# A decoder's attention kernel on one core: where the row-maxima blocks stand between TensorE's other blocks, and over how many PSUM banks they go

## The chip, the core and the metric

The kernel runs on one core of a Trainium2 chip. The metric is the device time in microseconds (us), the median of three runs. One further execution was taken by the hardware profiler; its trace is what the rows below show. TensorE is called PE (PEld is its weight load), VectorE DVE, ScalarE ACT, GpSimd POOL, and SyncE SP.

## What is computed

Two decoder layers with a layer norm ahead of each part, on x of 4 x 512 x 256:

```
x = x + self_attention0(norm(x))      # 16 heads of 16, all 512 keys, bias min(slope*(q-k), 8)
x = x + cross_attention0(norm(x), ctx, mask)   # 8 heads of 64, 1601 keys, keys masked
x = x + mixture0(norm(x))
x = x + attention1(norm(x))           # over the 4 batch entries, causal
x = x + cross_attention1(norm(x), ctx)         # 16 heads of 64, 1601 keys, no mask
x = x + mixture1(norm(x))

sim = q @ k.T * scale ;  attn = softmax(sim, -1) ;  out = (attn @ v) @ Wo + bo
```

All is float32; the softmax needs the maximum over the keys for each query row.

## The kernel before, in words

Each stage is a block in which every engine runs its own hand-written instruction list, and the engines meet at semaphores. An engine takes its list strictly in order, so an instruction that waits holds up all that stands behind it.

In both attention kinds the scores are computed twice. First, with the queries on the partitions, only for the row maximum: PE writes scores into a bank MB, DVE reduces the bank to one number per query. These are the **maxima**. Later, with the keys on the partitions and minus the maximum folded into the product as one more row, for the softmax: PE writes **scores** into one of three banks SB, ACT takes the exponential into a ring PR, PE multiplies PR with the values into OB (the **values**). The maxima of a group run while the scores of the group before it are worked on.

**Self attention** (`self_attention`): 256 score tiles n of 128 x 512, 16 of them are a group (4 heads, 4 query tiles). The loop over n has on PE: scores n (L617), the jobs of `at(n)`, the maxima of tile n + 22 (L581) and, at each fourth n, the values (four products side by side, L593). At n % 16 == 6 PE turns the finished output of the group before (L601) in its own bank OB. DVE's loop has a band subtraction on part of the scores (L751), the jobs, the maxima (L720 with a bias strip, L723 without) and, at n % 16 == 8, the division. Jobs are the projections "p" and "v", the row job that turns the maxima, and "a" and "o" for the output; they share the one bank JB, and each waits until the one before has been read. Banks: three SB, two MB, two OB, one JB.

**Cross attention** (`cross`, layer 0 masked with 4 pairs of heads, layer 1 without mask and 8 pairs): a group g is one pair of heads of one batch entry, 16 groups in layer 0 and 32 in layer 1. A group has 14 steps t over its 13 key tiles. On PE a step is: scores of head 0 and head 1 (L1077 and L1078 each), the jobs of `at(g, t)`, one **couple** of maxima, the values of the step before (L1093), and another couple. A couple is the maxima matmul (L1050) of head 0 into MB[0] and that of head 1 into MB[1], 400 keys wide, for one query tile. A group needs 16 couples, two in each step t = 3 to 10, for the group after. On DVE a step is the jobs, the four reductions (L1217 masked, L1220 not), then at t = 3 to 6 one quarter of the reciprocal of the sums (L1227), with the product (L1231) behind the last. Jobs: "k" (L1009, ACT copies the high half, DVE subtracts for the low half, L1191) at t = 0 to 3, "q" at 0, "sum" at 2, "v" (L1021, ten matmuls) from 4 on in most groups, "out" (L1036) at 8 and 9, "row" (L1025) at 11. Not every step has a "v" job: in layer 1 an even group has it at t = 4 to 7, an odd one at 4 to 6; for the last two pairs of a batch entry (an even and an odd group) all seven lie in the odd one. The groups 6, 14, 22 and 30 of layer 1 and 2, 6, 10 and 14 of layer 0 thus have no job at t = 4 to 7. Layer 0 also prepares the next batch entry's mask on DVE in three groups. PE may write a maxima bank once DVE has reduced what was in it: maxima m waits for reduction m - 2.

## Times and profile before

| | us |
|---|---|
| median of 3 runs | 3410.16 |
| lowest, highest | 3408.29, 3428.79 |
| the profiled execution | 3417.53 |
| its span in the trace | 3415.8 |
| mean granted TensorE clock, share of full | 0.926 |

| engine | busy us | share of the span |
|---|---|---|
| PE | 2995.6 | 88% |
| PEld | 1748.6 | 51% |
| DVE | 1934.0 | 57% |
| POOL | 1675.4 | 49% |
| ACT | 1274.2 | 37% |

A busy PE is one with a matmul in its pipeline; the ends are modelled, so the start of a matmul against the start of the next says more than its duration. Self attention lies at about 160 to 560 us of the span, the masked cross attention at 600 to 1500, the other one at 1700 to 3275.

### The profile page before, as it was taken

The page shows a single profiled execution, that of the slowest core. Times are in us where ns is not written, and L with a number is a line of the kernel's source. Part 1 is how long each engine was busy: PE and PEld are TensorE (multiplying, and loading weights), DVE is VectorE, ACT ScalarE, POOL GpSimd, SP SyncE. Part 2 cuts the span into 40 slices and gives each one's busy share as a digit, 9 for nine tenths or more (in the row PEclk, how much of TensorE's full clock was granted, in tenths as well). Part 3 has the DMA queues.
Part 4 walks back from the last instruction along what each step waited for, and adds up shares of the span by engine and source line. Part 5 has one row for each costly group of instructions (what it writes and reads, how often), then busy time and mean ns, then how long its engine had stood idle before and what let it go on. Part 6 is the DMA issues. An engine that isn't in the chain of part 4 may idle for free. (4 is left out here: it accounts for less than half of the span.)

```text
span 3415.8 us, 38759 instructions
## 1 busy us (share of the span) xinstructions
PE 2995.6 (88%) x12634; PEld 1748.6 (51%) x12634; DVE 1934.0 (57%) x4250; ACT 1274.2 (37%) x2299; POOL 1675.4 (49%) x1408
## 2 busy tenths in 40 slices
PE   6578886889999899768589999999999999999979
PEld 5223333555555455354355555555555555555557
DVE  2455664565665665443555665565556555655546
ACT  1144443434344344311144444444444444444420
POOL 0344202355555656530246665666656666666620
PEclk8778886999999999888599999999999999999979
DMA  8756501233132222100222232222312223222110
GB/s 270 149 158 152 114 1 61 66 93 71 40 94 65 74 69 51 37 0 0 65 64 57 70 94 57 56 70 62 91 48 70 68 55 84 70 62 54 40 50 25
DMA packets 113536, 245.84 MB, mean 72 GB/s; under 512 B 15366, under 2 KB 61703, under 8 KB 112184
## 3 DMA queue, kind: packets, MB, share of 16 engines
q1 hardware_dynamic: 107128, 219.82, 25.6%
q0 software_dynamic: 5696, 23.42, 2.5%
q8 instruction: 102, 1.67, 0.2%
q14 instruction: 98, 0.80, 0.1%
q10 hardware_dynamic: 512, 0.13, 0.0%
HBM read 107.31 MB, written 31.76 MB: 41 GB/s over the span
## 5 line engine op out<-in xcount | busy, mean ns | idle before, releaser
L991 POOL TENSOR_TENSOR ACC<-ACC,PR 128x512 f32<-128x512 f32 (+1 forms) x1056 | 1346.1, 1296 | 636.6 <-ACT PR L1162 636.4
L1162 ACT ACTIVATE PR<-bank 128x512 f32<-128x512 f32 (+1 forms) x832 | 452.1, 595 | 783.5 <-PE bank L1078 780.1
L1093 PE MATMUL bank<-PR,V 128*64 128x512 f32 (+1 forms) x2496 | 665.5, 616 | 0.9 <-ACT OT L1148 0.7
L1050 PE MATMUL bank<-KH,QZ 128*128 128x400 f32 (+1 forms) x1536 | 529.3, 404 | 113.8 <-DVE mx L1220 57.4
L1220 DVE TENSOR_REDUCE mx<-bank 128x1 f32<-128x400 f32 (+1 forms) x1024 | 538.8, 567 | 145.5 <-PE bank L1050 134.2
L1077 PE MATMUL bank<-QA,KA 128*128 128x512 f32 (+1 forms) x1248 | 534.5, 428 | 4.6 <-DMA QB<-ROW 4.6
L1050 PEld LDWEIGHTS bank<-KH,QZ 128*128 128x128 f32 x1536 | 269.7, 190 | 503.9 <-DVE mx L1220 306.1
L1191 DVE TENSOR_TENSOR KB<-bank,KH 64x400 fp32r<-64x400 f32 (+1 forms) x384 | 219.6, 572 | 531.0 <-ACT KH L1121 527.3
L1078 PE MATMUL bank<-QB,KB 65*128 65x512 f32 (+1 forms) x1248 | 498.2, 399 | 0.0
L1162 ACT ACTIVATE PR<-bank,keybias 128x512 f32<-128x512 f32 (+1 forms) x416 | 264.3, 683 | 406.7 <-PE bank L1078 395.7
L1077 PEld LDWEIGHTS bank<-QA,KA 128*128 128x128 f32 (+1 forms) x1248 | 232.9, 187 | 213.5 <-issue 94.7
L1217 DVE CUSTOM_DVE_ANT_0 bank<-bank,maskadd 128x400 f32<-128x400 f32 (+1 forms) x512 | 284.8, 593 | 66.6 <-PE bank L1050 63.9
L991 POOL TENSOR_TENSOR ACC<-PR 128x512 f32<-128x512 f32 x96 | 121.4, 1284 | 289.8 <-ACT PR L1162 289.8
L1078 PEld LDWEIGHTS bank<-QB,KB 65*128 65x128 f32 (+1 forms) x1248 | 233.7, 187 | 41.8 <-issue 11.0
L1093 PEld LDWEIGHTS bank<-PR,V 128*64 128x64 f32 (+1 forms) x2496 | 128.3, 135 | 203.1 <-issue 131.0
L1021 PEld LDWEIGHTS bank<-WV,CX 128*128 128x128 f32 (+1 forms) x1560 | 209.2, 188 | 15.1 <-issue 0.4
L1009 PE MATMUL bank<-CX,WK 128*128 128x400 f32 (+1 forms) x960 | 209.6, 349 | 8.4 <-DVE KB L1191 5.4
L1021 PE MATMUL bank<-WV,CX 128*128 128x256 f32 (+1 forms) x1560 | 214.9, 283 | 0.0
L679 ACT ACTIVATE PR<-bank 128x512 f32<-128x512 f32 x256 | 146.3, 598 | 183.2 <-DVE bank L751 130.1
L1227 DVE RECIPROCAL RD<-RD 128x128 f32<-128x128 f32 x192 | 180.0, 942 | 47.6 <-ACT RD L1113 46.7
L1009 PEld LDWEIGHTS bank<-CX,WK 128*128 128x128 f32 x960 | 180.5, 191 | 26.6 <-DVE KB L1191 6.7
L1205 DVE TENSOR_TENSOR X<-bank,X 128x512 f32<-128x512 f32 x96 | 66.4, 691 | 152.3 <-PE bank L1036 152.3
(228 smaller groups left out, 3110.0 us busy)
## 6 DMA issues: line engine op xcount, KB each, us to landing
KA<-KH SPq DMA_DIRECT2D x192, 400.5 KB, 6.3
CX<-ctx_split SPq DMA_DIRECT2D x8, 2403.0 KB, 10.6
WK<-wk_split SPq DMA_DIRECT2D x48, 256.0 KB, 5.7
WV<-wv_split SPq DMA_DIRECT2D x24, 512.0 KB, 3.6
QA<-QZ SPq DMA_DIRECT2D x96, 128.0 KB, 2.3
QB<-QZ SPq DMA_DIRECT2D x96, 128.0 KB, 2.4
first<-in_w_in SPq DMA_DIRECT2D x8, 1024.0 KB, 6.3
second<-in_w_out1T SPq DMA_DIRECT2D x8, 1024.0 KB, 8.8
```

The source lines that it names most:

```text
L991: pool.tensor_tensor(acc, other, PR[0:r, n % RING, :], ALU.add).then_inc(summed, 1)
L1009: last = pe.matmul(J[:, 0:w], W[:, u, :], CX[:, v, o:o + w], start=(n == 0), stop=(n == 4))
L1021: last = pe.matmul(J[0:r, o:o + 2 * P], CX[:, v, t * P:t * P + r], WV[:, u, :], start=(n == 0), stop=(n == 4))
L1050: pe.matmul(MB[h][:, 0:w], QZ[:, h, t * P:(t + 1) * P], KH[:, o:o + w], start=True, stop=True).then_inc(mx_ready, 1)
L1077: pe.matmul(SB[n % 3][0:r, :], KA[:, par, h, t * P:t * P + r], QA[:, par, h, :], start=True, stop=False)
L1078: pe.matmul(SB[n % 3][0:r, :], KB[:, par, h, t * P:t * P + r], QB[:, par, h, :], start=False, stop=True).then_inc(sc_ready, 1)
L1093: last = pe.matmul(OB[h * DH:(h + 1) * DH, :], V[0:r, g % 4, s, h * DH:(h + 1) * DH], PR[0:r, (n + h) % RING, :], start=(s == 0), stop=(s ...
L1162: act.activation(PR[0:r, n % RING, :], SB[n % 3][0:r, :], ACT.Exp, bias=keybias[0:r, g // pairs, t:t + 1] if masked else 0.0).then_inc(pro ...
L1191: last = dve.tensor_tensor(KB[0:DH, par, h, o:o + w], J[hd, 0:w], KH[hd, o:o + w], ALU.subtract)
L1217: dve.tensor_tensor_reduce(MB[h][:, 0:w], MB[h][:, 0:w], maskadd[:, g // pairs % 2, o:o + w], 1.0, -BIG, ALU.add, ALU.max, out).then_inc(m ...
L1220: dve.tensor_reduce(out, MB[h][:, 0:w], AX.X, ALU.max).then_inc(mx_done, 1)
L1227: dve.reciprocal(part, part).then_inc(inverted, 1)
```

## The change

One PSUM tensor `banks` of eight banks takes the place of eight tensors; `bank[i]` is a slice of it. Then:

- Self attention: three banks for the maxima (maxima m waits for reduction m - 3) and one OB in place of two. The turning of a finished output becomes a job "turn" in the bank JB, at n % 16 == 6, ahead of that step's maxima in place of behind them; the division reads JB and stands one step earlier on DVE. The values of a group wait until ACT has copied the output of the group before. The "p" jobs stand at 1, 3, 17, 19 of a batch entry's 64 steps (2, 5, 18, 21 before), the second "o" pair at 25 and 29 (24 and 26).
- Cross attention: the 32 maxima of a group stand in steps 2 to 9 (3 to 10 before), four in a step. Masked: one behind the scores of head 0, one behind those of head 1, one behind the jobs, one behind the values. Not masked: a pair between the scores of the two heads and a pair behind the jobs, none behind the values; DVE takes both heads by one reduction over the two banks (128 x 2 x 400), and PE waits for the reduction of the pair before. DVE has two of its reductions (masked) or one (not masked) ahead of the jobs of the step, the rest behind.

```
-        self.bank = [ctx.enter_context(nc.psum_tensor(f"bank{i}", [P, 512], F32)) for i in range(8)]
+        self.banks = ctx.enter_context(nc.psum_tensor("banks", [P, 8, 512], F32))
+        self.bank = [self.banks[:, i, :] for i in range(8)]
...
-        SB, MB, OB, JB = bank[0:3], bank[3:5], bank[5:7], bank[7]
+        SB, MB, OB, JB = bank[0:3], bank[3:6], bank[6], bank[7]
...
+            if n % GN == 6 and n >= GN:
+                jobs.append(("turn", n // GN - 1, 0))
...
-                        if m >= 2:
-                            pe.wait_ge(mx_done, m - 1)
+                        if m >= 3:
+                            pe.wait_ge(mx_done, m - 2)
...
-                        if t == 0 and g >= 2:
-                            pe.wait_ge(o_done, g - 1)
+                        if t == 0 and g >= 1:
+                            pe.wait_ge(o_raised, g)
...
-        def couples(g, t):
+        def singles(g, t):
 
-            return [(g + 1, i) for i in range(2 * (t - 3), 2 * (t - 2))] if g + 1 < G and 3 <= t <= 10 else []
+            return [(g + 1, i, h) for i in range(2 * (t - 2), 2 * (t - 1)) for h in range(2)] if g + 1 < G and 2 <= t <= 9 else []
...
+                        m = 2 * (NT * NC * g + i) + h
+                        turn = m // 2 if h == 0 and not masked else m - 1
...
+                        if m >= 2 and (masked or h == 0):
+                            pe.wait_ge(mx_done, turn)
+                        pe.matmul(MB[h][:, 0:w], QZ[:, h, t * P:(t + 1) * P], KH[:, o:o + w],
+                                  start=True, stop=True).then_inc(mx_ready, 1)
...
+                                for x in singles(g, t)[h:h + 1] if masked else singles(g, t)[0:2 - 2 * h]:
+                                    maximum(*x)
                             for x in at(g, t):
                                 job(x)
-                            for x in couples(g, t)[0:1]:
-                                maxima(*x)
+                            for x in singles(g, t)[2:3] if masked else singles(g, t)[2:4]:
+                                maximum(*x)
...
-                                dve.tensor_reduce(out, MB[h][:, 0:w], AX.X, ALU.max).then_inc(mx_done, 1)
+                            dve.tensor_reduce(mx[:, :, t, c], both[:, :, 0:w], AX.X, ALU.max).then_inc(mx_done, 1)
```

PE in the second cross attention, an odd group, steps 7 and 8 (no "v" job in step 7), before. KH, QZ are the maxima; QA, KA and QB, KB the scores; PR, V the values; WO, OT the "out" job:

```order
L1077 MATMUL bank<-QA,KA 128x512
L1078 MATMUL bank<-QB,KB 128x512
L1077 MATMUL bank<-QA,KA 128x512
L1078 MATMUL bank<-QB,KB 128x512
L1050 MATMUL bank<-KH,QZ 128x400 x2
L1093 MATMUL bank<-PR,V 64x512 x2
L1050 MATMUL bank<-KH,QZ 128x400 x2
L1077 MATMUL bank<-QA,KA 128x512
L1078 MATMUL bank<-QB,KB 128x512
L1077 MATMUL bank<-QA,KA 128x512
L1078 MATMUL bank<-QB,KB 128x512
L1036 MATMUL bank<-WO,OT 128x256 x2
```

The same step 7 and the start of step 8 in the change:

```order
L1074 MATMUL banks<-QA,KA 128x512
L1075 MATMUL banks<-QB,KB 128x512
L1046 MATMUL banks<-KH,QZ 128x400 x2
L1074 MATMUL banks<-QA,KA 128x512
L1075 MATMUL banks<-QB,KB 128x512
L1046 MATMUL banks<-KH,QZ 128x400 x2
L1092 MATMUL banks<-PR,V 64x512 x2
L1074 MATMUL banks<-QA,KA 128x512
L1075 MATMUL banks<-QB,KB 128x512
L1046 MATMUL banks<-KH,QZ 128x402 x2
```

Between the two pairs of a step there were the values; now there is one head's scores and the job, if there is one, and the values lie between the second pair and the next step.

DVE in the second cross attention, from the "k" job of step 3 to the end of step 7, before. KB is the subtraction of the "k" job, mx the reductions, RD and OT the reciprocal and the product:

```order
L1191 TENSOR_TENSOR KB<-bank,KH 64x402 x2
L1220 TENSOR_REDUCE mx<-bank 128x1 x4
L1227 RECIPROCAL RD<-RD 128x128
L1220 TENSOR_REDUCE mx<-bank 128x1 x4
L1227 RECIPROCAL RD<-RD 128x128
L1220 TENSOR_REDUCE mx<-bank 128x1 x4
L1227 RECIPROCAL RD<-RD 128x128
L1220 TENSOR_REDUCE mx<-bank 128x1 x4
L1227 RECIPROCAL RD<-RD 128x128
L1231 TENSOR_TENSOR OT<-OT,RD 128x512
L1220 TENSOR_REDUCE mx<-bank 128x1 x4
L1205 TENSOR_TENSOR X<-bank,X 128x512
```

In the change:

```order
L1190 TENSOR_TENSOR KB<-banks,KH 64x402 x2
L1220 TENSOR_REDUCE mx<-banks 128x2
L1227 RECIPROCAL RD<-RD 128x128
L1220 TENSOR_REDUCE mx<-banks 128x2 x2
L1227 RECIPROCAL RD<-RD 128x128
L1220 TENSOR_REDUCE mx<-banks 128x2 x2
L1227 RECIPROCAL RD<-RD 128x128
L1220 TENSOR_REDUCE mx<-banks 128x2 x2
L1227 RECIPROCAL RD<-RD 128x128
L1231 TENSOR_TENSOR OT<-OT,RD 128x512
L1220 TENSOR_REDUCE mx<-banks 128x2 x3
```

Four reductions of one bank became two of two banks; the first of step 3 now stands ahead of the "k" job, and the first "out" addition behind the first pair of step 8.

PE in self attention around the turning of an output, before (QS, KS with L617 scores, KS, QS with L581 maxima):

```order
L617 MATMUL bank<-QS,KS 128x512
L581 MATMUL bank<-KS,QS 128x512
L601 MATMUL bank<-ident,RAISED 128x128 x4
L617 MATMUL bank<-QS,KS 128x512
L581 MATMUL bank<-KS,QS 128x512
L593 MATMUL bank<-PR,SV 32x512 x4
```

In the change:

```order
L617 MATMUL banks<-QS,KS 128x512
L570 MATMUL banks<-ident,RAISED 128x128 x4
L587 MATMUL banks<-KS,QS 128x512
L617 MATMUL banks<-QS,KS 128x512
L587 MATMUL banks<-KS,QS 128x512
L599 MATMUL banks<-PR,SV 32x512 x4
```

The turning moved from behind the maxima to ahead of them.

## Rows read from the trace of the kernel before

**Rows 1.** Stages in the windows view: length, engines' busy us (instructions), TensorE clock, DMA

```profile
160.00:560.00 400.00, 329.00 (x1305) 132.81 (x1305) 226.81 (x629) 176.33 (x321) 103.44 (x124) 0.78 0.41 96
600.00:1500.00 900.00, 807.74 (x3421) 477.68 (x3421) 530.31 (x1396) 371.37 (x623) 516.35 (x411) 0.95 0.25 62
1700.00:3275.00 1575.00, 1493.77 (x6544) 874.58 (x6544) 921.66 (x1590) 655.00 (x1227) 985.08 (x781) 1.00 0.27 65
```

**Rows 2.** Timeline, second cross attention, one ordinary step: start us, duration, instruction

```profile
2624.42 0.64 PE L1050 MATMUL bank<-KH,QZ 128*128 128x400 f32 x2
2624.89 0.39 PE L1077 MATMUL bank<-QA,KA 128*128 128x512 f32 x1
...
2625.83 1.34 PE L1021 MATMUL bank<-WV,CX 128*128 128x256 f32 x10
2625.88 0.94 DVE L1227 RECIPROCAL RD<-RD 128x128 f32<-128x128 f32 x1
...
2627.00 0.53 PE L1050 MATMUL bank<-KH,QZ 128*128 128x400 f32 x2
2627.39 1.05 DVE L1220 TENSOR_REDUCE mx<-bank 128x1 f32<-128x400 f32 x2 [0.56 <-PE bank L1050]
2627.46 1.08 PE L1093 MATMUL bank<-PR,V 128*64 128x512 f32 x4
2628.47 0.45 PE L1050 MATMUL bank<-KH,QZ 128*128 128x400 f32 x1
```

**Rows 3.** Timeline, step 3 of a group: the reductions behind the "k" job

```profile
2619.45 2.18 DVE L1220 TENSOR_REDUCE mx<-bank 128x1 f32<-128x400 f32 x4
...
2620.09 0.93 PE L1050 MATMUL bank<-KH,QZ 128*128 128x400 f32 x2 [1.02 <-DVE mx L1220]
2620.86 0.39 PE L1077 MATMUL bank<-QA,KA 128*128 128x512 f32 x1
```

**Rows 4.** Timeline, step 7 of an odd group, behind reciprocal and product

```profile
2585.47 1.08 PE L1093 MATMUL bank<-PR,V 128*64 128x512 f32 x4
2585.94 1.26 DVE L1231 TENSOR_TENSOR OT<-OT,RD 128x512 f32<-128x512 f32 x1
2587.12 2.16 DVE L1220 TENSOR_REDUCE mx<-bank 128x1 f32<-128x400 f32 x4
2587.74 0.93 PE L1050 MATMUL bank<-KH,QZ 128*128 128x400 f32 x2 [1.19 <-DVE mx L1220]
```

**Rows 5.** Timeline, the second couple of step 9 and the "row" job of step 11

```profile
2644.81 0.89 PE L1050 MATMUL bank<-KH,QZ 128*128 128x402 f32 x2
...
2600.81 0.30 PE L1025 MATMUL bank<-ident,MT 128*128 128x128 f32 x1 [0.36 <-DVE MT L1237]
```

**Rows 6.** Groups by form: busy us, mean ns of one, idle before

```profile
L1220 DVE TENSOR_REDUCE mx<-bank 128x1 f32<-128x400 f32 x768 | 403.7, 567 | 107.3 <-PE bank L1050 99.1
L723 DVE TENSOR_REDUCE MT<-bank 128x1 f32<-128x512 f32 x80 | 54.0, 684 | 3.7 <-PE bank L581 2.9
```

**Rows 7.** Windows around step 7 of two masked groups without "v" jobs; columns as in Rows 1

```profile
755.00:759.00 4.00, 2.47 (x10) 0.96 (x10) 3.95 (x9) 1.26 (x2) 3.24 (x3) 1.00 0.90 341
759.00:763.00 4.00, 4.00 (x13) 2.97 (x13) 1.31 (x5) 1.37 (x2) 2.06 (x2) 0.57 0.12 50
1173.00:1177.00 4.00, 2.44 (x10) 0.99 (x10) 3.95 (x9) 1.15 (x2) 2.99 (x3) 1.00 0.86 351
1177.00:1181.00 4.00, 3.92 (x17) 2.27 (x16) 2.84 (x10) 1.27 (x2) 2.51 (x2) 1.00 0.04 14
```

**Rows 8.** Timeline, self attention, one block of four scores

```profile
348.55 0.50 PE L617 MATMUL bank<-QS,KS 63*128 63x512 f32 x2
349.32 0.70 DVE L720 CUSTOM_DVE_ANT_0 bank<-bank,strip 128x512 f32<-128x512 f32 x1 [0.89 <-PE bank L581]
...
352.20 0.50 PE L617 MATMUL bank<-QS,KS 63*128 63x512 f32 x2
```

**Rows 9.** Waits within 160 to 560 us: total us, times, longest

```profile
DVE bank L720 <- PE bank L581: 31.1, 38, 2.3
PE bank L581 <- DVE MT L720: 27.4, 43, 1.9
```

94 lines of the change are left out of this document (43 added, 51 removed).

## The prediction

> **What bounds the kernel now.** I read the windows view by stage first. In the second cross attention PE is busy 1494 of 1575 us at a clock of 1.00, in the masked one 808 of 900 at 0.95, in self attention 329 of 400 at 0.78 [rows 1]; DVE stands at 53 to 59% in all three. So PE's list, in its order, sets the length, and DVE matters only where PE waits for it. The next view is the timeline of one ordinary step of the second cross attention. By starts, it is: the second couple of the step before 0.47 us, two heads' scores 0.94, the "v" job 1.17, the first couple 0.46, the values 1.01; 4.05 in all [rows 2]. Four reductions and a reciprocal, 1.05 + 1.05 + 0.94, are done meanwhile, so there is no wait. The waits sit in a few steps of each group:
>
> - Step 3: DVE first does the subtraction of the "k" job. The second couple waits 1.02 us, to which 0.07 belongs that the modelled end of the values covers (they last 1.08 but free PE after 1.01), and its two matmuls take 0.77 in place of 0.47: 1.4 us lost [rows 2, 3].
> - Step 7 of an odd group, which has no "v" job: behind the fourth reciprocal and the product of 1.26 the values' start and the couple's lie 2.27 apart instead of 1.01. With the slower couple that is 1.6 us [rows 4]. With a "v" job of 1.17 in that step 0.4 is left.
> - Steps 8 and 9: the couple lasts 0.89 in place of 0.64, 0.25 us each; step 11: the row job idles 0.36 for the last maxima [rows 2, 5].
>
> **One reduction over two banks.** The trace has none, but a reduction of 400 takes 567 ns and one of 512 takes 684 [rows 6], 1.04 ns an element, so 800 should take 567 + 417 = 984 ns. The bounds are 833 (elements at that rate alone) and 1134 (two of today's); I take 0.98. Its successor starts 0.08 earlier than its end, as behind the product [rows 4].
>
> The Trainium skill ("VectorE: DVE Perf Modes", the section on the TRN2 errata) says that each instruction pays a fixed cost and gives 120 cycles plus one an element at 0.96 GHz for a PSUM source, so one reduction in place of two would save 0.125 us a pair. The row of 567 ns is 25 ns above that formula.
>
> What counts for PE is another thing. A matmul starts about 0.06 us after the reduction that frees its bank (2619.45 + 0.57 = 2620.02, the couple at 2620.09) [rows 3], and before, head 0's bank was free after the first 0.57. Now both banks stay closed until the one reduction is done. With the first matmul of a pair at 0, the second at 0.18 (I take half of an undisturbed pair without a change of block kind, 0.36), a reduction starts 0.39 behind its matmul [rows 2], at 0.57, ends at 1.55, and the next pair can start at 1.61. PE reaches the second pair of a step after 0.36 + 0.47 for the pair and one head's scores, plus the job: at 0.83 + job. From the second pair to the first of the next step there are 0.46 + 1.01 + 0.57 (scores behind values pay 0.1 for the change of kind that the couple pays now) = 2.04 us, always enough unless DVE is busy otherwise.
>
> **Second cross attention, step by step.**
> - Steps with a "v" job of 1.17: 2.00 against 1.61, no wait, 4.05 as before.
> - Step 3 to 4: DVE starts the second pair's reduction where it starts the first one's today, at 2619.45 [rows 3]; the first couple stood at 2617.53 (2620.09 less the wait of 1.02, the values' 1.08 and the couple's 0.46), so that is 1.92 after the "k" job. It ends at 2.91, and the next pair is due at 2.04: 0.93 lost plus 0.1 for the spread of the pair. Gain 0.36 a group.
> - Step 7: behind step 6's second pair DVE has 0.57 + 0.90 (reduction), 0.98 (reciprocal, start to start), 1.19 (product, 2585.94 to 2587.12 [rows 4]); the two-bank reduction starts at 3.64 and ends at 4.62, the next pair starts at 4.68. PE is there at 2.04 + 0.83 + job: with a "v" job 0.64 + 0.1 lost against 0.4; without one 1.8 + 0.1, and 0.3 in step 6 with its half job, against 1.6. Loss 0.35 or 0.6 a group.
> - Steps 8 and 9: 0.4 a group gained. Step 11: 0.36 gained, since the maxima end two steps earlier. The maxima that move from step 10 to step 2 stand between blocks of the other kind there and cost 0.35 more in changes of kind.
> - Groups 6, 14, 22, 30 have no "v" job in steps 4 to 7: each of these steps waits 1.61 - 0.83 = 0.8 + 0.1 (step 4 some 0.3 more), where today they lose about 0.15. That is 2.1 us a group in sum with the other terms.
> - The 16 couples of the first group run alone: two of them with a "v" job take 1.61 + 0.36 + 1.17 = 3.14, at least 2 x 1.61 = 3.2; today four reductions and the waits, some 2.95. Loss 2 us.
>
> Sum: 15 groups with a job in step 7 gain 0.4 (6), 12 odd groups gain 0.1 (1), 4 lose 2.1 (8), 2 at the start: 3 us longer.
>
> **The clock.** In step 7 without a job PE will be idle about 1.8 us. In the masked stage two such steps leave PE busy 2.47 and 2.44 us in 4; after one of them the clock falls to 0.57 in the next 4 us, after the other it stays [rows 7]. That stage's mean is 0.95. In the second cross attention it never falls, with waits like that of [rows 4] in it. With 4.68 us between two second pairs of which 2.87 are work, the new step is emptier than both kinds, and it comes 12 + 4 = 16 times. I take 11 falls. One fall costs at most 4 x 0.43 = 1.7 us [rows 7], less where PE waits anyway: 1.5. That is 16 us, bounds 0 and 27.
>
> **Masked cross attention.** Reductions stay single; only the places change. Step 3's 1.4 shrinks to 0.7, steps 8 and 9 and the row job gain about as above; but the third maxima matmul is now due before the values, 1.0 us earlier against DVE, so steps without a job wait for DVE's reciprocal: four groups lose 1.6, eleven gain 0.4 to 1.2. Sum 2 us gained, and two falls of the clock more (3 us): 1 us longer, bounds -6 and +8.
>
> **Self attention.** In a block of four scores, 3.65 us, DVE idles 0.89 because PE, between the values of 1.0 us, can put only two maxima ahead [rows 8]. A third bank lets it put three: 3 x 0.65 us of DVE work against about 1.8 until the next arrives. DVE's waits of this kind sum to 31 us, and PE's waits the other way to 27 [rows 9]. Not all return: in blocks with projections or at half clock PE itself is the slow one. I take 22 us gained, bounds 0 and 50 (64 blocks by 0.8). What it costs: the turning now stands ahead of the maxima and waits for ACT's copy, and it shares JB. If DVE had nothing in store that is up to 0.7 us in 15 groups, 10 us; with the third bank it has something in store. The moves of "p" and "o" exchange places of equal work: nothing, cover being the exponentials of three banks. No DMA is moved or added.
>
> **Sum.** -22 + 3 + 16 + 1 = -2 us against the profiled execution's 3417.5 us, which stands 0.2% above the median of 3410.2. So 3408.
>
> **Rivals.** About 1% (34 us) is what a measurement of this kernel can tell from no change.
> - *No change beyond 1%*, as forecast: chance 0.62, 3376 to 3444, its likely part 3385 to 3430.
> - *Self attention was bound by the two banks all over*: each block gives back 0.7, 45 us, and steadier work lifts its clock of 0.78. For it: 0.89 idle of DVE in 3.65. Against it: that wait occurs 38 times, not 64. Time 3410 - 45 + 20 = 3385, with the clock 3370. Chance 0.16.
> - *The saved fixed cost comes out in the end*: 512 x (2 x 0.567 - 0.984) = 77 us of DVE work, time 3335. Against it: DVE is 59% busy and has no wait in the ordinary step. Chance 0.03. This is what the skill's rule on fixed costs suggests; its own figure would give 512 x 0.125 = 64 us, as an estimate.
> - *Slower: the two-bank reduction makes the clock fall.* If all 16 step-7 waits and the waits of 0.9 us in the four poor groups bring falls, each costing 1.7 and a late restart of DVE's work, some 30 falls make 51 us, time 3410 - 13 + 51 = 3448 with half the gain in self attention. It decides from about 25 falls on. For it: the emptier step. Chance 0.12.
> - *The one output bank and the turn job hold self attention up*, no gain there: 3430 at 10 us of loss and all else as forecast. Chance 0.07, inside 1% for the most part.
>
> Faster 0.2, same 0.66, slower 0.14. The range 3372 to 3440 leaves out the second rival's lower end, the third and the fourth.
>
> **What would show it.** In the changed profile: a two-bank reduction of 980 ns; in step 7 of odd groups a PE wait of 1.8 us behind the scores, not behind the values; clock below 1.00 between 1700 and 3275; ordinary steps of 4.05 us; no DVE idle of 0.9 behind the values in self attention and a stage some 20 us shorter; a row job without a wait. Wrong would be the prediction if the ordinary step changed its length, since it comes some 150 times, or if self attention moved by more than 40 us.

## The result and the profile after

| | before | after |
|---|---|---|
| median, us | 3411.14 | 3354.52 |
| lowest, highest | 3408.29, 3428.79 | 3353.41, 3356.66 |
| span of the profiled execution | 3415.8 | 3351.8 |
| granted TensorE clock | 0.926 | 0.932 |

The ratio is 0.9837, with a 95% interval of 0.9803 to 0.9871: 1.6% faster. The forecast was 3408, with a range down to 3372. The time lies below the range.

The stages can be told apart by starts: self attention from its first exponential to its last, a cross attention from the row job of its first group to that of its last. The profiled executions give:

| us | before | after | change | forecast |
|---|---|---|---|---|
| self attention | 365.2 | 325.1 | -40.1 | -22 |
| masked cross attention | 767.8 | 764.1 | -3.7 | +1 |
| between the cross attentions | 336.3 | 342.6 | +6.3 | +2 |
| second cross attention | 1506.1 | 1483.3 | -22.8 | +17 |
| the rest | 440.4 | 436.7 | -3.7 | 0 |

The stretch between ends with the row job of the second cross attention's first group, so it holds that group's 16 couples, which run alone (the forecast's "2 at the start" stands here). From the first maxima matmul of that group to its row job, in the windows view (columns: window, length, PE, PEld, DVE, ACT and POOL busy, granted clock, DMA share, GB/s), before and after:

```profile
1700.00:1726.10 26.10, 20.27 (x98) 15.09 (x98) 18.58 (x35) 3.96 (x7) 8.54 (x13) 0.87 0.49 117
1651.20:1683.30 32.10, 20.68 (x97) 16.18 (x97) 17.56 (x19) 3.96 (x7) 8.51 (x13) 0.79 0.40 96
```

PE is busy as long as before and the stretch is 6 us longer. It takes 32.1 to 32.2 us in every run below whose second cross attention reduces two banks at once, and 26.0 to 26.2 us in every other one. So the 6.3 us belong to the two-bank reduction; 2 were forecast. The half clock that falls into it, 6.8 us before and 13.6 after, is part of that.

The stage windows, which answer to [rows 1] (same columns):

```profile
160.00:520.00 360.00, 289.06 (x1305) 121.57 (x1304) 227.36 (x642) 174.81 (x322) 103.89 (x124) 0.87 0.45 108
560.00:1460.00 900.00, 796.73 (x3412) 473.65 (x3412) 548.40 (x1412) 380.64 (x622) 517.27 (x411) 0.95 0.24 61
1650.00:3210.00 1560.00, 1483.41 (x6544) 861.65 (x6544) 869.98 (x1078) 680.38 (x1229) 972.67 (x783) 0.99 0.27 65
```

Self attention's clock rose from 0.78 to 0.87; the second cross attention's, where 11 falls were forecast, is 0.99, and this window also takes in 10 us of half clock around the stage's start.

Groups by form, second cross attention (busy us, mean ns of one, idle before), for [rows 6]:

```profile
L1220 DVE TENSOR_REDUCE mx<-banks 128x2 f32<-128x800 f32 x370 | 365.3, 987 | 155.5 <-PE banks L1046 152.6
L1220 DVE TENSOR_REDUCE mx<-banks 128x2 f32<-128x802 f32 x124 | 122.8, 990 | 60.3 <-PE banks L1046 60.3
```

The two-bank reduction takes 0.987 us; 0.984 was worked out. The Trainium skill ("VectorE: DVE Perf Modes", the section on the TRN2 errata) would give (120 + 800) / 0.96 = 958 ns as an estimate, 3% below the row.

Step 7 of an odd group, without a "v" job, for [rows 4] (timeline: start, duration, instruction, idle before and what ended it):

```profile
1858.86 0.94 DVE L1227 RECIPROCAL RD<-RD 128x128 f32<-128x128 f32 x1
...
1859.83 0.69 DVE L1231 TENSOR_TENSOR OT<-OT,RD 128x512 f32<-128x512 f32 x1
...
1860.37 2.50 POOL L987 TENSOR_TENSOR ACC<-ACC,PR 128x512 f32<-128x512 f32 x2 [1.24 <-ACT PR L1161]
1860.44 0.98 DVE L1220 TENSOR_REDUCE mx<-banks 128x2 f32<-128x800 f32 x1
...
1861.48 0.63 PE L1046 MATMUL banks<-KH,QZ 128*128 128x400 f32 x2 [1.07 <-DVE mx L1220]
1862.05 1.08 PE L1092 MATMUL banks<-PR,V 128*64 128x512 f32 x4
```

PE waits behind the scores, as forecast, but 1.07 us and not 1.8, since the product lasts 0.69 us and not 1.26. The wait behind the "k" job, for [rows 3], and the row job, for [rows 5] (same timeline):

```profile
1846.37 0.99 DVE L1220 TENSOR_REDUCE mx<-banks 128x2 f32<-128x800 f32 x1
...
1847.51 0.60 PE L1046 MATMUL banks<-KH,QZ 128*128 128x400 f32 x2 [0.86 <-DVE mx L1220]
...
1873.76 0.27 PE L1021 MATMUL banks<-ident,MT 128*128 128x128 f32 x1
```

By the starts of the exponentials, the steps of a group of the second cross attention last (median over the groups of a kind, us; "poor" are 6, 14 and 22, without "v" jobs; "single" is the kernel of e7_single_reduce, below):

| step | 2 | 3 | 4 | 5 | 6 | 7 | 8 | 9 | 10 | 11 | group |
|---|---|---|---|---|---|---|---|---|---|---|---|
| even, before | 3.93 | 5.18 | 4.04 | 4.05 | 4.04 | 4.57 | 3.99 | 3.99 | 2.88 | 2.73 | 49.07 |
| even, after | 4.97 | 3.81 | 5.14 | 4.05 | 4.05 | 4.20 | 3.76 | 3.76 | 2.14 | 2.20 | 47.72 |
| even, single | 4.97 | 3.79 | 4.97 | 4.05 | 4.05 | 4.05 | 3.74 | 3.74 | 2.14 | 2.20 | 47.34 |
| odd, before | 3.90 | 5.17 | 4.06 | 4.04 | 3.45 | 4.54 | 3.99 | 4.00 | 2.88 | 2.73 | 48.39 |
| odd, after | 4.98 | 3.80 | 5.14 | 4.04 | 3.75 | 4.21 | 3.77 | 3.76 | 2.14 | 2.18 | 47.43 |
| odd, single | 4.98 | 3.79 | 4.97 | 4.05 | 3.45 | 3.97 | 3.74 | 3.72 | 2.14 | 2.18 | 46.63 |
| poor, before | 3.93 | 5.18 | 3.00 | 3.04 | 3.00 | 4.55 | 4.00 | 3.99 | 2.88 | 2.73 | 45.96 |
| poor, after | 4.97 | 3.81 | 4.90 | 3.75 | 3.75 | 4.22 | 3.76 | 3.76 | 2.14 | 2.20 | 46.92 |
| poor, single | 4.97 | 3.79 | 4.86 | 3.46 | 3.45 | 3.66 | 3.75 | 3.74 | 2.14 | 2.20 | 45.67 |

The ordinary step with a job did not change (4.05).

Self attention: one block of the bias-strip kind, from the score that ends the block before it to the one that ends it, for [rows 8] (timeline):

```profile
339.48 0.50 PE L617 MATMUL banks<-QS,KS 63*128 63x512 f32 x2
...
340.25 0.70 DVE L717 CUSTOM_DVE_ANT_0 banks<-banks,strip 128x512 f32<-128x512 f32 x1 [0.29 <-PE banks L587]
...
342.48 0.50 PE L617 MATMUL banks<-QS,KS 63*128 63x512 f32 x2
```

The block takes 3.00 us (3.65 before), with 0.29 of DVE idle where 0.89 was. The waits of the stage (total us, times, longest), for [rows 9]:

```profile
PE banks L570 <- ACT RAISED L662: 25.2, 13, 3.6
DVE banks L717 <- PE banks L587: 21.6, 32, 1.5
...
PEld banks L587 <- DVE MT L717: 9.8, 25, 3.0
...
PE banks L587 <- DVE MT L717: 2.6, 1, 2.6
```

PE's wait for the reductions fell from 27.4 us to 2.6, and that of its weight loads, which overlaps with it, from the 55.8 of this row of before to 9.8:

```profile
PEld bank L581 <- DVE MT L720: 55.8, 65, 2.6
```

In their place stands the turn job's wait for ACT's copy, 25.2 us. These rows alone don't say from which of the change's parts the 40 us come.

The clock fell once between 1700 and 3160 us, in step 4 of group 22, a poor one (windows, columns as above), for [rows 7]:

```profile
2754.60:2758.60 4.00, 2.47 (x10) 1.26 (x8) 3.44 (x5) 1.19 (x2) 2.08 (x3) 1.00 0.88 178
2758.60:2762.60 4.00, 4.00 (x12) 1.83 (x10) 2.03 (x3) 0.56 (x1) 0.96 (x1) 0.57 1.01 228
```

That group took 48.5 us, the three like it 46.9: a fall costs 1.6 us, as forecast (1.5). But there was one, not 11, and it came in step 4 of a group without "v" jobs and not in a step 7.

### The profile page after: what moved, and what is told of

Its sections match the earlier page's. It is cut to its first block and busy times, and to the rows that moved or that the text cites. A ratio compares the mean times of both kernels' runs of the same rounds, so it can differ in the third digit from the quotient of the medians.

```text
span 3351.8 us, 38244 instructions
## 1 busy us (share of the span) xinstructions
PE 2940.3 (88%) x12634; PEld 1724.7 (51%) x12634; DVE 1892.8 (56%) x3738; ACT 1304.6 (39%) x2299; POOL 1663.3 (50%) x1408
## 3 DMA queue, kind: packets, MB, share of 16 engines
q1 hardware_dynamic: 107128, 219.82, 26.2%
## 5 line engine op out<-in xcount | busy, mean ns | idle before, releaser
L1161 ACT ACTIVATE PR<-banks 128x512 f32<-128x512 f32 (+1 forms) x832 | 478.6, 596 | 732.8 <-PE banks L1075 726.4
L1092 PE MATMUL banks<-PR,V 128*64 128x512 f32 (+1 forms) x2496 | 672.8, 622 | 0.9 <-ACT OT L1147 0.7
L1220 DVE TENSOR_REDUCE mx<-banks 128x2 f32<-128x800 f32 (+1 forms) x512 | 506.0, 988 | 230.2 <-PE banks L1046 227.3
L1046 PE MATMUL banks<-KH,QZ 128*128 128x400 f32 (+1 forms) x1536 | 500.1, 381 | 129.1 <-DVE mx L1220 63.4
L1074 PE MATMUL banks<-QA,KA 128*128 128x512 f32 (+1 forms) x1248 | 560.1, 449 | 4.6 <-DMA QB<-ROW 4.6
L1075 PE MATMUL banks<-QB,KB 65*128 65x512 f32 (+1 forms) x1248 | 497.7, 399 | 0.0
L1046 PEld LDWEIGHTS banks<-KH,QZ 128*128 128x128 f32 x1536 | 273.1, 192 | 368.5 <-issue 141.6
L1161 ACT ACTIVATE PR<-banks,keybias 128x512 f32<-128x512 f32 (+1 forms) x416 | 272.9, 686 | 373.5 <-PE banks L1075 352.4
L1217 DVE CUSTOM_DVE_ANT_0 banks<-banks,maskadd 128x400 f32<-128x400 f32 (+1 forms) x512 | 291.5, 586 | 92.2 <-PE banks L1046 87.6
L1075 PEld LDWEIGHTS banks<-QB,KB 65*128 65x128 f32 (+1 forms) x1248 | 233.5, 187 | 24.9 <-issue 11.0
L1227 DVE RECIPROCAL RD<-RD 128x128 f32<-128x128 f32 x192 | 180.1, 943 | 51.5 <-ACT RD L1112 50.6
```

Source lines behind the costliest of these rows:

```text
L1046: pe.matmul(MB[h][:, 0:w], QZ[:, h, t * P:(t + 1) * P], KH[:, o:o + w], start=True, stop=True).then_inc(mx_ready, 1)
L1074: pe.matmul(SB[n % 3][0:r, :], KA[:, par, h, t * P:t * P + r], QA[:, par, h, :], start=True, stop=False)
L1075: pe.matmul(SB[n % 3][0:r, :], KB[:, par, h, t * P:t * P + r], QB[:, par, h, :], start=False, stop=True).then_inc(sc_ready, 1)
L1092: last = pe.matmul(OB[h * DH:(h + 1) * DH, :], V[0:r, g % 4, s, h * DH:(h + 1) * DH], PR[0:r, (n + h) % RING, :], start=(s == 0), stop=(s ...
L1161: act.activation(PR[0:r, n % RING, :], SB[n % 3][0:r, :], ACT.Exp, bias=keybias[0:r, g // pairs, t:t + 1] if masked else 0.0).then_inc(pro ...
L1217: dve.tensor_tensor_reduce(MB[h][:, 0:w], MB[h][:, 0:w], maskadd[:, g // pairs % 2, o:o + w], 1.0, -BIG, ALU.add, ALU.max, out).then_inc(m ...
```

## The experiments

### Which part, which stage

`e1_self_only` takes the function of self attention from the change, `e2_cross_only` that of the cross attention.

```
 # e1_self_only: self_attention of after, all else of before
-        SB, MB, OB, JB = bank[0:3], bank[3:5], bank[5:7], bank[7]
+        SB, MB, OB, JB = bank[0:3], bank[3:6], bank[6], bank[7]
...
 # e2_cross_only: cross of after and the one tensor, all else of before
+        both = self.banks[:, 4:6, :]
...
```

> The kernel before with the self attention of the change; both cross attentions as before. Theory A (the parts are independent; the traces put 45 us of the 64 into the part before the first cross group): 3411 - 45 = 3366 us. Rival (the self attention gives only the forecast 22 us, the rest of the early gain comes from elsewhere): 3389 us.

> The change with the self attention of before. Theory A: the second cross attention gains 23 us, the masked one 4, the stages between lose 6: 3411 - 20 = 3391 us, product of step 6 in layer 1 at 0.69 us in every group. Rival (the cross part is what I forecast, and its gain hangs on the shifted start): 3411 +- 5 us, or a product of 1.3 us again.

Measured: the first 3375.7 us (3371.4 to 3380.7), ratio 0.990 (0.986 to 0.994); self attention 329 us, the second cross attention 1506 as before. The other 3398.7 us, ratio 0.998 (0.995 to 1.000), self attention 367 and the second cross attention 1483, as in after. Their stages are those of the change: the profiles show no action of the one part on the other. The times are less exact. The first lies between its theory (3366) and its rival (3389), and the two ratios make 1.2%, 42 us, where the change has 1.6%, 56 us; the intervals allow both. Most of the gain is self attention's.

### Self attention: the bank, the jobs' places, the division

`e3_two_banks` is the changed kernel with two maxima banks; `e8_old_jobs` has its "p" and "o" jobs at the old places.

```
-                        if m >= 3:
-                            pe.wait_ge(mx_done, m - 2)
-                        pe.matmul(MB[m % 3][:, :], ...
+                        if m >= 2:
+                            pe.wait_ge(mx_done, m - 1)
+                        pe.matmul(MB[m % 2][:, :], ...
```

> The change, but the maxima of self attention use two of their three banks and wait for reduction m - 2 again. Theory A (the third bank is what makes self attention faster): blocks of four scores without a band take 3.65 us again in place of 3.0, the stage is 35 to 45 us longer than in the change, time about 3393. Rival B (the new places of the jobs and the turn job do it): less than 15 us longer.

> The change with the projection jobs of self attention at 2, 5, 18, 21 and the output jobs at 24 and 26 as before. Theory A: equal work exchanges places, within 5 us of the change. Rival B (the jobs' places carry a good part): 10 to 25 us longer than the change.

Measured: 3364.6 us with two banks, the stage 338 us; the quiet blocks are back at 3.6 us, and still the stage is 27 us shorter than before. The theory that the bank gives all, which was my forecast's, missed, and its rival (less than 15 us) holds. The jobs' places are worth nothing that one execution can tell: 3350.9 us, stage 324.

So what is left was taken apart. `e9_norm_earlier` is the kernel before with one number changed; `e10_norm_old` is e3_two_banks with that number put back; `e11_turn_behind` is e3_two_banks with the turning behind the maxima.

```
 # e9_norm_earlier (e10_norm_old the other way round)
-                        if n % GN == 8 and g >= 1:
+                        if n % GN == 7 and g >= 1:
                             normalise(g - 1)
```

> The kernel before, with one thing taken from the change: in self attention VectorE divides a group's outputs one score earlier (behind the maxima of score 7 of 16 instead of 8). Self attention, from its first exponential to its last, took 365 us before and 325 after, and 338 with two maxima banks and all else of the change; so some 27 us of its gain are not the third bank. Theory N: the division stood right ahead of the maxima that TensorE wanted next, and its earlier place is what gives the 27 us: 338 to 345 us here, in all about 3385. Theory T: the turning of the outputs ahead of the maxima, and not the division, gives them: within 5 us of 365 here, in all 3400 to 3415.

> The changed kernel with two maxima banks in self attention, and with the division of a group's outputs back at its old place (score 8 of 16); the turning stays ahead of the maxima. With the division at score 7 the stage took 338 us. Theory N: back to 360 or more, in all 3385. Theory T: within 5 us of 338, in all 3360 to 3368. If the two work only together, something between here and in the next run too.

> The changed kernel with two maxima banks in self attention, and with the turning of the outputs behind the maxima of score 6, as before the change; the division stays at score 7. Theory T: self attention back from 338 to 360 us or more, in all 3385. Theory N: within 5 us of 338, in all 3360 to 3368.

Measured: 3381.2, 3412.3 and 3368.1 us; the stage 339, 385 and 344. Theory N (the division's place) holds in the first, and in the last but for half a us. The second moved by more than it said. With the turned output in the shared bank, a late division also keeps that bank closed for the row job. Its waits show that (total us, times, longest), a row that neither before nor after has; how much of the 20 us beyond before it explains is open, since half-clock time rose too, to 214 us:

```profile
PEld banks L566 <- DVE A L730: 10.8, 10, 1.1
```

Here is the mechanism, before, in the timeline of group 7 of 0 to 15, its scores 8 to 11:

```profile
357.05 2.21 ACT L679 ACTIVATE PR<-bank 128x512 f32<-128x512 f32 x4 [1.06 <-PE bank L617]
...
357.84 0.25 DVE L732 RECIPROCAL small<-bank 128x16 f32<-128x16 f32 x1
...
358.13 0.42 DVE L735 TENSOR_TENSOR A<-bank,small 128x256 f32<-128x256 f32 x1
358.47 0.69 DVE L720 CUSTOM_DVE_ANT_0 bank<-bank,strip 128x512 f32<-128x512 f32 x1
...
359.36 0.38 PE L563 MATMUL bank<-ident,MT 128*16 128x128 f32 x2 [0.83 <-DVE MT L720]
...
360.23 1.93 PE L593 MATMUL bank<-PR,SV 128*32 128x512 f32 x8
...
362.10 0.80 PE L617 MATMUL bank<-QS,KS 63*128 63x512 f32 x2
...
362.98 0.60 ACT L679 ACTIVATE PR<-bank 128x512 f32<-128x512 f32 x1 [2.94 <-PE bank L617]
```

and the same place in e9_norm_earlier:

```profile
346.51 0.25 DVE L732 RECIPROCAL small<-bank 128x16 f32<-128x16 f32 x1
...
346.80 0.42 DVE L735 TENSOR_TENSOR A<-bank,small 128x256 f32<-128x256 f32 x1
...
347.38 2.22 ACT L679 ACTIVATE PR<-bank 128x512 f32<-128x512 f32 x4 [1.06 <-PE bank L617]
347.55 0.70 DVE L720 CUSTOM_DVE_ANT_0 bank<-bank,strip 128x512 f32<-128x512 f32 x1 [0.33 <-PE bank L581]
...
349.11 0.38 PE L563 MATMUL bank<-ident,MT 128*16 128x128 f32 x2 [0.24 <-DVE MT L720]
...
349.83 1.07 PE L593 MATMUL bank<-PR,SV 128*32 128x512 f32 x8
...
350.83 0.50 PE L617 MATMUL bank<-QS,KS 63*128 63x512 f32 x2
...
351.64 0.60 ACT L679 ACTIVATE PR<-bank 128x512 f32<-128x512 f32 x1 [1.86 <-PE bank L617]
```

The division is 0.67 us of DVE in both. At score 8 it stands between two reductions for which the row job of score 11 waits: 0.83 us of idle PE in place of 0.24. Behind that idle time the clock halves: the values take 1.93 us instead of 1.07, the scores 0.80 instead of 0.50. Together that is 0.6 + 0.9 + 0.3 = 1.8 us in this group. From one block's first exponential to the next one's, 357.05 to 362.98, it is 5.93 us; in the other kernel, 347.38 to 351.64, 4.26: 1.7 less. At score 7 the same 0.67 us lies where DVE has no full bank to reduce anyway. Not each of the 15 divisions costs that much. By the same starts, all blocks of scores 8 to 11 together take 97 us before and 83 in e9_norm_earlier, the blocks behind them (12 to 15) 82 and 74, and the rest 185 and 181: 26 us in all, and the half-clock time in the stage fell from 140 to 83 us. The self attention of before also stands in `e2_cross_only` and `e4_thin_before` (below), where it takes 367 and 356 us, and scores 8 to 11 take 97 and 94. So the single execution of e9_norm_earlier shows a gain of 17 to 27 us, 11 to 14 of it in the blocks with the division.

The stage as in after spreads from 325 to 337 us over the profiled executions of eight kernels that share it (mean 331; the profile of after is at the short end), and that of before from 356 to 367, so the bank was measured in more executions: `e14_two_banks_timed` is e3_two_banks again, and `e15_bank_alone` is the changed kernel with three banks, the division at 8 and the turning behind.

```
 # e15_bank_alone, against after
                         for x in at(n):
-                            job(x)
+                            if x[0] != "turn":
+                                job(x)
                         if n + LEAD < N:
                             maxima(n + LEAD)
+                        for x in at(n):
+                            if x[0] == "turn":
+                                job(x)
...
-                        if n % GN == 7 and g >= 1:
+                        if n % GN == 8 and g >= 1:
```

> The changed kernel with two maxima banks in self attention instead of three, all else of the change in place, measured again in rounds because the one look (3364.6 us, stage 338) lies at the edge of the spread of the changed stage (324 to 337 in six looks). Theory: the third bank is worth some 0.6 us in each of ten to fifteen quiet blocks, 8 us: 3362 to 3366. Forecast: 35 to 45 us, 3390 or more. Rival: nothing, 3350 to 3358.

> The changed kernel with the third bank, but with the division at its old place (score 8) and the turning behind the maxima, as before the change. It is the bank alone, as far as self attention goes. Theory N: the division at its old place stands ahead of the reductions that the row job needs, and a third bank can't help: self attention 350 to 365 us, in all 3380 to 3395. Forecast: the bank is what gave the gain, 325 to 335 us, 3355 to 3365.

Measured: 3371.1 us (3359.2 to 3379.4) without the bank, the stage 342; 3386.2 us (3371.4 to 3397.0) with the bank alone, the stage 352, where Theory N put it. Against after's 3354.5 the bank is worth some 17 us by the times, or 9 by the stages (331 against 338 and 342), and the earlier division, together with the turning's place, 32 by the times, or 21 by the stages (by e11_turn_behind 2 to 5 us of it may be the turning's). Bank alone: 352 against 356, 365 and 367, so 4 to 15 us. By the means, 363 and 331, the stage gained 31 us and not the 40 of the two profiles. How it splits is settled to some 10 us only; the stage's own spread, which goes along with its half-clock time (53 to 93 us), hides the rest.

### The cross attentions: the product and GpSimd

The product OT x RD lasts 1.26 us in [rows 4] and 0.69 in after. What runs beside it, before, is this row of POOL:

```profile
2585.38 2.94 POOL L991 TENSOR_TENSOR ACC<-ACC,PR 128x512 f32<-128x512 f32 x2 [0.94 <-ACT PR L1162]
```

The product starts at 2585.94, 0.56 into the first of two additions, which takes 1.27 and ends at 2586.65; the product ends at 2587.20, 0.55 behind that. The pair of additions takes 2.94 us instead of the 2.50 of the row of after above, where the product starts on an idle POOL. It looks as if the two exclude each other. `e4_thin_before` and `e5_thin_after` shorten the additions to 8 columns (most of the sums are left out; the product's input differs, not its size):

```
-                                acc = ACC[0:r, g % 2, h, :]
+                                acc = ACC[0:r, g % 2, h, 0:8]
...
-                                pool.tensor_tensor(acc, other, PR[0:r, n % RING, :], ALU.add).then_inc(summed, 1)
+                                pool.tensor_tensor(acc, other, PR[0:r, n % RING, 0:8], ALU.add).then_inc(summed, 1)
```

> The kernel before, with GpSimd's additions of the probabilities over 8 columns instead of 512, so that GpSimd is idle nearly always; most of the sums are left out and the output is not the reference's. Theory A: VectorE's product of 512 columns from SBUF to SBUF lasts longer while an addition on GpSimd runs: 1.30 us in the second cross attention of the kernel before falls to about 0.69, 1.38 in the masked one to about 0.7, and the odd groups of the second cross attention get 0.5 us shorter (49.05 to 48.5), some 8 to 15 us in all. Rival: the product's length comes from something else, such as its wait: 1.3 us as before, no change of the groups.

> The changed kernel with the same thin additions on GpSimd (output not the reference's). Theory A: the second cross attention's product is at 0.69 us already, so that stage stays within 4 us of 1483; the masked stage's product falls from 1.65 to 0.7 and that stage gets 5 to 15 us shorter (764). Rival: product 1.65 in the masked stage as before.

(The groups of 49.05 us are the even ones; the expectation calls them odd.) Measured, one execution each: 3349.9 and 3326.6 us, and the product is 0.69 us in every group of both kernels. The second cross attention of before takes 1489.1 us instead of 1506.1, all of it in step 7 (4.57 to 4.05, and 4.54 to 3.98); the masked one 744.6 instead of 767.8. With the change the second one stays at 1483.3 and the masked one falls from 764.1 to 740.8. So 17 us of the change's gain in the second cross attention come from a meeting that no longer happens. In the masked one the meetings cost 23 us before and 23 us after.

Not all of these 23 us are the product's, and they are more than the 5 to 15 expected. 6 us of them in after (7 before) lie in step 5 of the three groups that prepare the mask. There DVE copies the mask's rows (`CAST maskadd<-mask_rows`, 128x1601), and the copy takes 1.93 us in after, 2.01 before and 1.00 in both kernels with the thin additions: it meets them too. Nearly all of the rest, 17 us in after, is step 7, some of it through the clock, which falls there in groups 13 and 14 of after and not in e5_thin_after.

The Trainium skill ("SBUF — State Buffer", the section "Who interferes with whom") says it: a VectorE instruction with two inputs in SBUF contends with a GpSimd instruction that reads SBUF, and the one issued first has the port for its whole length. The trace agrees, 1.26 us against 0.69. My prediction took 1.26 from the row, did not ask what was in it, and kept it for the changed kernel.

`e12_product_later` moves the product from behind the fourth reciprocal to between the two pairs of maxima of step 7, in both layers; `e6_more_dve` adds a reciprocal of 64 columns behind it in the second one.

```
 # e12_product_later
                             for x in at(g, t):
                                 job(x)
+                            if g >= 1 and t == 3 + NT:
+                                invert(g - 1, NT)
                             for x in singles(g, t)[2:4]:
...
-                        if i == NT - 1:
+                        if i == NT:
...
 # e6_more_dve
                             dve.tensor_tensor(OT[:, :], OT[:, :], RD[:, :], ALU.mult).then_inc(normed, 1)
+                            if not masked:
+                                dve.reciprocal(self.small[:, 0:64], ones[:, 0:64])
```

> The changed kernel with one move in both cross attentions: VectorE multiplies the outputs by the reciprocals not behind the fourth reciprocal, ahead of the first maxima of the next step, but between that step's two pairs of maxima. In the second cross attention TensorE waits for that backlog: in step 7 without a job its two pairs stand 1.36 us too far apart by the sum (first reduction starts 3.18 after the pair of step 6, ends 4.17), with the product behind it the reduction ends at 3.60 and the second pair loses 0.8. Theory A: 0.56 us less in 12 odd groups and in the 4 poor ones, 0.2 in the 15 with a job there: 12 us less in the second cross attention (1483 to 1471), 0 to 8 in the masked one, in all 3354 to about 3340. Rival: the product in its new place runs beside an addition on GpSimd and takes 1.3 to 1.6 us instead of 0.69, which then delays the second reduction; no gain, 3350 to 3360.

> The changed kernel with one more instruction on VectorE behind the product of the second cross attention, a reciprocal of 64 columns (some 0.5 us estimated) once a group. It restores the longer product that my forecast had, and with it the idle time of 1.8 us of TensorE in step 7 that was to bring a fall of the clock. Theory A: groups without a job in step 7 get 0.5 us longer by the wait alone (47.7 to 48.2; 12 odd and 4 poor ones), the 15 with a job 0.3 to 0.5: 1483 to about 1491; clock falls come in few groups, at most 4. Rival, the forecast: 11 or more falls of 1.5 us, 1483 to 1505 or more, with a granted clock below 0.99 for the stage.

Measured for e12_product_later: 3331.4 us (3323.6 to 3338.9). The masked cross attention takes 734.7 us, 29 less; more than the "0 to 8" expected, because the product there met an addition in after. In a group with jobs and without mask parts step 7 takes 5.62 us in after, 4.67 with the thin additions and 4.05 here: 0.95 us are the meeting, 0.6 the place. Masked, after:

```profile
917.45 2.94 POOL L987 TENSOR_TENSOR ACC<-ACC,PR 128x512 f32<-128x512 f32 x2 [1.42 <-ACT PR L1161]
917.62 1.64 DVE L1231 TENSOR_TENSOR OT<-OT,RD 128x512 f32<-128x512 f32 x1
...
919.87 0.45 PE L1046 MATMUL banks<-KH,QZ 128*128 128x400 f32 x1 [2.46 <-DVE mx L1217]
```

Masked, e12_product_later:

```profile
915.78 2.95 POOL L987 TENSOR_TENSOR ACC<-ACC,PR 128x512 f32<-128x512 f32 x2 [1.41 <-ACT PR L1161]
...
916.51 0.45 PE L1046 MATMUL banks<-KH,QZ 128*128 128x400 f32 x1 [0.78 <-DVE mx L1217]
...
916.84 0.75 DVE L1232 TENSOR_TENSOR OT<-OT,RD 128x512 f32<-128x512 f32 x1
```

PE's wait falls from 2.46 to 0.78 us; the product meets only the end of an addition (0.75 us). In the second cross attention the rival came true: at the new place the product meets an addition (1.31 us), and the stage takes 1485.6 us, 2 more. The even and odd groups did get 0.16 and 0.32 us shorter. The four poor ones ate that up, each with a fall of the clock in step 4: two take 50.6 us instead of 46.9, with 10.2 us of half clock each, the other two 48.2. Why the clock falls there more often than in after is open.

e6_more_dve: 3369.5 us, the stage 1500.1. The groups got 0.4 us longer, 12 us in all, and there were 4 falls of the clock (after: 1), three of them in step 7, at 1.6 to 1.8 us each. With the longer wait the place and the price of a fall are those of the forecast; the number would have been wrong even so.

### One reduction over two banks against two

`e7_single_reduce` has the places of the change, and in the second cross attention a reduction of its own for each head.

```
-                        turn = m // 2 if h == 0 and not masked else m - 1
+                        turn = m - 1
...
-                        if m >= 2 and (masked or h == 0):
+                        if m >= 2:
...
-                            dve.tensor_reduce(mx[:, :, t, c], both[:, :, 0:w], AX.X, ALU.max).then_inc(mx_done, 1)
+                            dve.tensor_reduce(out, MB[h][:, 0:w], AX.X, ALU.max).then_inc(mx_done, 1)
```

> The changed kernel, but in the second cross attention each head's maxima are reduced by an instruction of their own (567 ns each in place of one of 988), at the places of the change. Theory A: the gain of 23 us there (1506 to 1483) comes from the places (maxima that end two steps earlier, the pairs that leave steps 8 to 10) and from the product of 0.69 us; what the one reduction saves on VectorE (1024 instructions fewer, some 75 us of its time) is worth little, because in ordinary steps TensorE does not wait: 1478 to 1490 us in the stage here, 3345 to 3362 in all. Rival: VectorE's backlog in steps 3 to 7 is what PE waits for; there are nine to twelve pairs a group behind a backlog, each later by 0.15 us: 1500 us or more, 3370 in all.

Measured: 3332.5 us, and 1463.8 us for the stage, 19.5 less than with the one instruction and below what either theory said. The first group's couples ahead of the stage take 26.1 us again instead of 32.1, so the one instruction costs 25 us in all. Both lengths come back closely: the stage takes 1482.9 to 1483.4 us in nine profiled executions with the one instruction at the places of the change, and 1463.2 to 1463.8 in four with two. The gain sits where DVE was to profit (table above): step 4 from 5.14 to 4.97, steps without a job from 3.75 to 3.45, step 7 from 4.20 to 4.05 or 3.66. The timeline of step 7 of the same odd group shows why:

```profile
1855.68 0.69 DVE L1229 TENSOR_TENSOR OT<-OT,RD 128x512 f32<-128x512 f32 x1
...
1856.29 2.16 DVE L1218 TENSOR_REDUCE mx<-banks 128x1 f32<-128x400 f32 x4
...
1856.91 0.93 PE L1046 MATMUL banks<-KH,QZ 128*128 128x400 f32 x2 [0.54 <-DVE mx L1218]
1857.77 1.08 PE L1092 MATMUL banks<-PR,V 128*64 128x512 f32 x4
```

The reductions start at the same distance behind the product, 0.61 us. With one a bank, PE gets head 0's bank after 0.62 and the pair is through after 1.48, when the values start; with one over both it starts after 1.04 and the values after 1.61. The instruction saves 0.15 us of DVE (0.987 against 2 x 0.567) and keeps the first bank closed for 0.42 us more. What it took to make it pay, DVE as the bound, is not there: DVE waits 152.6 + 60.3 us for PE in that stage of after.

### The two findings together

`e13_best` is e7_single_reduce with the product moved in the masked layer alone. `e16_mask_late` also moves the mask's preparation, and `e17_mask_late_timed` is the same kernel in four more executions.

```
 # e13_best, against e7_single_reduce
-                        if i == NT - 1:
+                        if i == (NT if masked else NT - 1):
...
+                            if masked and g >= 1 and t == 3 + NT:
+                                invert(g - 1, NT)
 # e16_mask_late, against e13_best
-                            if masked and g % pairs == 1 and g // pairs + 1 < B and t in (4, 6, 8, 11):
+                            if masked and g % pairs == 1 and g // pairs + 1 < B and t in (9, 10, 11, 12):
```

> The changed kernel with the two findings of the runs so far: in the second cross attention one reduction a head instead of one over two banks (1463.8 instead of 1483.3 us there), and in the masked one the product between the two pairs of maxima of step 7 (734.7 instead of 764.1). Theory A: the two stages don't touch each other, so 20 and 29 us add up: second cross attention 1464, masked 735, in all 3354.5 - 19.5 - 29.4 = 3306, with self attention's spread 3295 to 3315. Rival: the stages are coupled by the clock, and the falls come elsewhere: 3315 to 3330.

> The kernel of e13_best, with the four parts of the mask's preparation (one copy of 1601 elements 1.9 us, one reduction of 1601 1.8 us, and small ones) that VectorE does in steps 4, 6, 8 and 11 of three groups of the masked cross attention moved to steps 9 to 12, of which 10 to 12 have no maxima. In those groups steps 5 and 7 take 6.1 to 7.6 and 7.7 us instead of 4.0 each, steps 8 0.9 more. Theory A: 5 to 6 us a group, 15 to 18 in all: masked stage 735 to 718, in all 3290. Rival: the parts delay the first subtractions of the next group by as much: within 4 us of e13_best.

> The kernel of e16_mask_late again, in rounds: the one look gave 3277.2 us, with e13_best at 3304.6 (3297.7 to 3307.7). Theory A (the three groups' waits for the mask's parts are gone, some 20 us): 3270 to 3290. Rival (the look was at the lower end of self attention's spread, and the move is worth 10 us or less): 3292 to 3300.

Measured: 3304.6 us (3297.7 to 3307.7), ratio to before 0.969 (0.962 to 0.976); stages 735.9 and 1463.2, so the two add up as expected. With the mask's parts moved the masked stage takes 714.8 us (step 7 of the three groups 3.9 us instead of 7.7, step 5 4.0 instead of 6.1 to 7.5), and the copy of the mask's rows 1.00 us instead of 1.93, since at its new place it meets no addition. The kernel takes 3277.2 us in a single execution and 3279.5 us (3278.6 to 3283.9) over four, ratio 0.9625 (0.958 to 0.967). Both kernels beat before and after.

## Why the prediction was wrong

By stage, the profiles lie 62 us below the sum: 40 in the second cross attention, 18 in self attention, 5 in the masked one and 4 in the rest; the stretch between is 4 longer than in the sum. Two steps of the working failed in the main.

- **The step that cost most: step 7 of the second cross attention.** The sum took the product at 1.26 us, as it stands in the row, over into the changed kernel. There it lasts 0.69. With 1.26 the wait became 1.8 us and step 7 was to cost 0.35 to 0.6 more; it took 1.07 us and gave 0.33 to 0.37. e4_thin_before puts the product's part at 17 us. The 11 falls of the clock, 16 us, hung on the same wait, and on the single masked step of [rows 7]. One came, of the kind that the slower rival added, in a group without "v" jobs; its price, 1.6 us, was right. e6_more_dve, with 0.4 us more, brought 4.
- **The step left out: the division of self attention.** My sum took the bank, the turning and the jobs, and has no term for the division at score 7 instead of 8, which the change's text names. It is the largest single part of self attention's gain, 17 to 27 us alone and 21 to 32 in the changed kernel. The bank, for which I took 22, gave 4 to 17. The rival "bound by the two banks all over" came nearest in number (45 us), for a reason that e3_two_banks refutes. That the clock would rise with steadier work was in that rival only; 0.78 became 0.87. The sign of being wrong that I had named, a move of over 40 us, stands at its edge: 40.1 in the two profiles, 31 by the means.
- **What bounds the kernel: right.** PE's list set the length of the second cross attention, and DVE mattered in the steps named. The ordinary step stayed at 4.05 us, and 75 us less of DVE work bought nothing there.
- **The loss from the turning came** (25.2 us of waits for ACT's copy), larger than the 10 us I allowed. What it costs at the end is small: with the turning behind the maxima the stage is no shorter (344 against 338 to 342).
- **The two-bank reduction: right in length and in its effect on the steps.** 0.987 us against 0.984; steps without a job 3.75 us each, where 0.9 us of wait on 3.0 was forecast. But nothing in the sum compares it with two reductions at the same places. By e7_single_reduce it costs 19.5 us in the stage and 6 in the first group ahead of it, for which the sum had 2.
- **The other terms of the second cross attention** were near. The row job gave 0.53 (forecast 0.36), steps 8 and 9 0.46 together (0.4), steps 3 and 4 together 0.27, and 0.46 with single reductions (0.36). The moved maxima cost 0.30 (0.35). With step 7 an even group gained 1.35, not 0.4; a poor one lost 0.96, not 2.1.
- **Masked cross attention:** -3.7 against +1. The product met an addition in both kernels, 1.3 to 1.57 us before and 1.64 in nearly all groups after, and by e4_thin_before and e5_thin_after the meetings cost 23 us in each. Without them the change is -3.8: groups with jobs and without mask parts gain 1.3 us, those without "v" jobs lose 1.2. That is the forecast's mechanism (0.4 to 1.2, and 1.6). That the meetings come out even is luck.
- **The slower rival** (two-bank reductions make the clock fall) had the right sign for the part and a far too large size.
- **Two slips of reading.** DVE stands at 57 to 59% in [rows 1], not 53 to 59. And the last maxima of a group move from step 10 to step 9, one step and not two.

The places with single reductions gave 42 us in the second cross attention (1506.1 to 1463.8): 17 by the product, and 25 by the new places of the maxima, which leave step 10 and end farther ahead of the row job. The one reduction took 19.5 of it back.

## What to carry to other kernels

Give each moved line of a change its own term, the smallest too: the division, 0.67 us between two reductions for which PE waited, cost 1.7 us in the group shown, two thirds of it through the clock, and one score earlier it lay in time in which DVE was idle anyway. Before a duration goes into a sum, look at what runs beside it: the same product lasts 0.69, 1.26 or 1.64 us by whether and since when GpSimd is adding, and a move can switch that on or off. And a merged instruction that saves time on an engine with slack can cost more where it keeps a buffer closed that the bounding engine waits for.

## What the runs showed of the hardware

- A VectorE tensor_tensor of 128x512 from SBUF lasts 0.69 us alone. Where a GpSimd addition of 1.27 us is already running, it ends 0.55 us after that addition does (0.75, 1.26 and 1.64 us in the rows), and the pair of additions takes 2.94 us instead of 2.50. With additions over 8 columns the effect is gone in all groups.
- A VectorE copy (CAST) of 128x1601 from uint8 to bfloat16 lasts 1.00 us beside the thin additions, and in e16_mask_late, and 1.93 to 2.02 us in before and after, where it meets an addition.
- An idle stretch of PE of 0.83 us in self attention was followed by half-clock values (1.93 us for 1.07); one of 0.24 was not. The half-clock time of that stage went from 140 us to 83 by one number in the code, and was 214 in e10_norm_old.
- A reduction over two banks, 128x800, costs 0.987 us, and two of 128x400 cost 1.134.
